# Mamba-2 layer in one kernel: other shapes for two TensorE products, a new order on every engine, and loads with a wait for each group

## The chip, the cores and the metric

The kernel runs on one core of one Trainium2 chip. The metric is the device time of that core in microseconds, from one launch.

## The reference

Two sequences of 4096 tokens, 256 wide (`x`, float32), go through a layer norm without weights; the result `xn` feeds two branches, and `x` is added to both:

```
zxbcdt = xn @ W_in                       # 256 -> 512 (z) + 768 (x, B, C) + 8 (dt)
xBC = silu(causal_conv(xBC, 4 taps))     # x: 8 heads of 64; B, C: 128 each
dt = softplus(dt + dt_bias); a = -exp(A_log)
y = ssd(x * dt, dt * a, B, C) + x * D    # the state space recurrence
y = y * silu(z); y = y * rsqrt(mean(y*y) + eps) * rms_w
h = xn + y @ W_out                       # 512 -> 256
branch1 = layernorm(h) * ln_g + ln_b
branch2 = tanh(xn @ F1 @ F2 @ F3 + bias)
out = x + branch1 + branch2
```

The reference cuts the recurrence into chunks of 64; the kernel uses chunks of 128 tokens, with the same result.

## The kernel before, in words

A step is 128 tokens of both sequences (`q` = 0 and 1), so there are 32 steps. Each engine has a program of its own; they meet at semaphores. Every program is a function `one_pass(k, b)` with the operations of several steps in an order written out by hand: step `k+2` is loaded and its statistics taken, `k+1` projected, `k` and `k-1` in the recurrence, `k-2` finished. Passes run from k = -2 to 33, the middle ones in a loop. An engine does its operations strictly in that order, and waits where one isn't ready.

For a step, TensorE transposes `xn` (`transpose_x`), projects the second branch and dt (`branch_project`), the six tiles of convolution channels (`conv_project`, ct = 0 to 5) and z (`z_project`). These are float32r products: each operand is split into a high and a low part, and three products of one pass each are summed (`split_products`). Everything else on TensorE is plain float32; one such matmul stands in the trace as two instructions. `ring0` and `ring1` are the two PSUM banks through which the projections go, so that each projection waits until an earlier one has been read: `z_project(k, 0)` for the taps of tile 3, `conv_project(k, 4)` for those of tile 1.

VectorE adds three of the four convolution taps (`tap`, L624), computes softplus of 16 columns in steps of one small instruction each (`softplus(k, b, i)`, L637 to L659, the series of `log1p` with `LOG_TERMS` terms; the last step writes `a_wide` and increments `a_done`), and the chunk's elementwise work: `weigh` (L677), `scale_off` (L683), `new_state` (L689), `add_diag` (L694), `apply_gate` (L698), `last_h` (L705). In the order before, the softplus steps stand one by one between large instructions. `sums` on TensorE waits for `a_done`; ScalarE's `sums`, VectorE's `low_rows`, GpSimd's `spread_rows` and TensorE's `exponents` follow from it.

Inside a chunk, `y_diag` multiplies for each of 8 heads the 128x128 weights `mm` (stationary) with 64 columns of `xdt` (moving) into `yd_bank`, tokens on the partitions. `x_tokens` turns x to tokens, ScalarE copies it to `xsb`, and `x_times_dt` makes `xdt` in 8 instructions. GpSimd makes `xw`, the skip term `xd = x * D`, adds it (`add_skip`, L467), decays the state, masks, and does the inverse square roots and the output (L491, L493). After the gate, `transpose_y` turns y, ScalarE copies it to `yts` (L916), and `out_project` multiplies it with `wo` in float32.

Ahead of the passes come 16 loads and the constants: all are issued by the SP queue, and VectorE, ScalarE, TensorE and GpSimd each first wait until every load but those of `x` has landed (`s_load` >= 16 * 17). Then the weights are split, F1 @ F2 @ F3 is multiplied out, and the tables of the exponents (`left`, `right`) are filled by VectorE. Only then does VectorE begin with the norm of step 0.

Of the kernel before, what the change touches and what calls it, by code (L numbers as in the profile page):

```python
# [29 lines left out]
P = 128  # L30
# [25 lines left out]
LOG_TERMS = 6  # L56
# [11 lines left out]
def program(nc, x, w_in, conv_w, conv_b, dt_bias, a_log, d_skip, rms_w, w_out, ln_g, ln_b,  # L68
# [6 lines left out]
    with ExitStack() as ctx:  # L75
# [6 lines left out]
        def sems(name, n):  # L82
# [3 lines left out]
        ring0, ring1, e_bank0, e_bank1, xt_bank, bg_bank, yoff_bank, yd_bank = [  # L86
            ctx.enter_context(nc.psum_tensor(n, [P, 512], F32))
            for n in ("ring0", "ring1", "e_bank0", "e_bank1", "xt_bank", "bg_bank", "yoff_bank", "yd_bank")]
# [6 lines left out]
        lay2 = sb("lay2", [P, 4 * Q * DI])  # L95
# [6 lines left out]
        mask = lay2[:, 0:QUAD * P].rearrange("p (j t) -> p j t", t=P)  # L102
        pair = lay2[:, QUAD * P:2 * QUAD * P].rearrange("p (j t) -> p j t", t=P)
        sel = lay2[:, 2 * QUAD * P:2 * QUAD * P + Q * H]
        f3s = lay2[:, 2 * QUAD * P + Q * H:2 * QUAD * P + Q * H + nf].rearrange("p (k n) -> p k n", k=KD)
        f23 = lay2[:, 2 * QUAD * P + Q * H + nf:2 * QUAD * P + Q * H + 2 * nf].rearrange("p (k n) -> p k n", k=KD)
# [3 lines left out]
        wo = sb("wo", [P, KI, D])  # L110
        rmsw = sb("rmsw", [P, KI])
# [3 lines left out]
        d_bc = sb("d_bc", [P, H])  # L115
        lng = sb("lng", [P, D])
# [40 lines left out]
        w16 = sb("w16", [P, Q * H])  # L157
# [3 lines left out]
        xsb = sb("xsb", [P, Q, DI])  # L161
# [7 lines left out]
        t1, t2, yg = (lay2[:, i * Q * DI:(i + 1) * Q * DI].rearrange("p (q n) -> p q n", q=Q) for i in range(3))  # L169
        junk = sb("junk", [P, Q, DI])  # L170
        ss = sb("ss", [P, Q])
        sse = sb("sse", [P, Q])
        rr = sb("rr", [P, Q])
        yts = sb("yts", [P, Q, KI, P])
# [8 lines left out]
        s_load = sem("s_load")  # L183
        s_gp = sem("s_gp")
        s_const = sem("s_const")
        s_high = sem("s_high")
        s_sel = sem("s_sel")
        s_split = sem("s_split")
# [11 lines left out]
        f_in_psum, f_read, z_in_psum, zt_done, gate_done = (sems(n, Q) for n in ("f_in_psum", "f_read", "z_in_psum", "zt_done", "gate_done"))  # L200
        c_in_psum, u_done = (sems(n, CT) for n in ("c_in_psum", "u_done"))
        th_done, xs_done = (sems(n, NG) for n in ("th_done", "xs_done"))
        tap_done = sems("tap_done", CT)
        halo_done, relu_done, ee_done = map(sem, ("halo_done", "relu_done", "ee_done"))
        soft = sem("soft")
        a_done, res_chain, res_done = map(sem, ("a_done", "res_chain", "res_done"))
        sums_in_psum, sums_read, rows_done, spread_done, w16_done, total_done = map(
            sem, ("sums_in_psum", "sums_read", "rows_done", "spread_done", "w16_done", "total_done"))
        (xt2_in_psum, xsb_done, xdt_done, xw_done, xd_done, sdec_done, bg_in_psum, bg_read, yoff_in_psum, t1_done,
         t2_done, st_in_psum, state_done, g_done, yd_in_psum, y_done, yg_done, ss_done, sse_done, rr_done, yt_in_psum, yts_done,  # L210
         o_in_psum, h_done, st2_done, mv2_done, ve2_done, rs2_done, shift2_done, hn_done, hg_done, out_done) = (
            sems(n, Q) for n in (
                "xt2_in_psum", "xsb_done", "xdt_done", "xw_done", "xd_done", "sdec_done", "bg_in_psum", "bg_read",
                "yoff_in_psum", "t1_done", "t2_done", "st_in_psum", "state_done", "g_done", "yd_in_psum", "y_done", "yg_done",
                "ss_done", "sse_done", "rr_done", "yt_in_psum", "yts_done", "o_in_psum", "h_done", "st2_done",
                "mv2_done", "ve2_done", "rs2_done", "shift2_done", "hn_done", "hg_done", "out_done"))
        e_in_psum, e_done, m_done = ([sems(f"{n}{q}_", 2) for q in range(Q)] for n in ("e_in_psum", "e_done", "m_done"))

        def begun(step):

            return not isinstance(step, int) or step >= 0

# [47 lines left out]
        def _(sp):  # L270
# [6 lines left out]
            for j in range(BUF):  # L277
                load(j, j, slice(j * P, (j + 1) * P))
            loads = [
                (win[:, :, :], w_in.rearrange("(k p) n -> p k n", p=P)),  # L280
                (f1s[:, :, :], f1t.rearrange("(k p) n -> p k n", p=P)),
                (f2s[:, :, :], f2t.rearrange("(k p) n -> p k n", p=P)),
                (f3s[:, :, :], f3.rearrange("(k p) n -> p k n", p=P)),
                (wo[:, :, :], w_out.rearrange("(k p) n -> p k n", p=P)),
                (rmsw[:, :], rms_w), (cw[:, :, :], conv_w.rearrange("(k p) n -> p k n", p=P)), (cb[:, :], conv_b),
                (a_neg[:, 0:H], a_log.partition_broadcast(P)),
                (a_neg[:, H:2 * H], a_log.partition_broadcast(P)), (d_bc[:, :], d_skip.partition_broadcast(P)),
                (lng[:, :], ln_g.partition_broadcast(P)), (lnb[:, :], ln_b.partition_broadcast(P)),
            ]
            for dst, src in loads:  # L290
                sp.dma_start(dst, src).then_inc(s_load, 16)
            sp.wait_ge(s_gp, 1)
            for row in (0, LO):
                sp.dma_start(brow[row:row + 1, 0:D], f_bias.rearrange("(a n) -> a n", a=1)).then_inc(s_load, 16)
                sp.dma_start(brow[row:row + 1, D:FB], dt_bias.rearrange("(a n) -> a n", a=1)).then_inc(s_load, 16)
# [4 lines left out]
            def one_pass(k, b, loads_on=True):  # L300
                b1 = (b + 1) % BUF
                if live(k + 1) and loads_on and live(k + 1 + BUF):
                    sp.wait_ge(res_done, k + 2)
                    load(k + 1 + BUF, b1, rows_of(k + 1 + BUF))
                if live(k - 1):
                    sp.wait_ge(out_done[0], k)
                    sp.wait_ge(out_done[1], k)
                    bo = (b - 1) % BUF
                    sp.dma_start(out_t[rows_of(k - 1), :, :], obuf[:, bo]).then_inc(stored[bo], 16)
# [12 lines left out]
        n_loads = 13 + 4  # L322


        @block.gpsimd
        def _(pool):
# [6 lines left out]
            g.memset(nhalf[:, :], -0.5).then_inc(s_gp, 1)  # L333
            g.memset(a_wide[:, :], 0.0).then_inc(s_gp, 1)
# [45 lines left out]
            pool.wait_ge(s_load, 16 * n_loads)  # L380
            pool.wait_ge(s_split, 1)

            def layer_norm_scale(k):
                pool.wait_ge(mv1_done, k + 1)
# [865 lines left out]
```

## Time and profile before

| | us |
|---|---|
| median of 3 runs | 858.38 |
| lowest, highest | 854.18, 859.85 |
| profiled execution | 857.2 |
| its span in the trace | 855.5 |

The profiled execution is 1.7 us longer than the span that the trace shows, and 1.2 us under the median. Its granted TensorE clock was 0.976 of full speed over the span. Of the engines' rows below, a busy time counts an instruction from its start to its end; neighbours on one engine overlap a little, so what an instruction costs in a row of them is the distance from start to start.

### The profile page before, as it was taken

Reading aid. Unit: us, or ns where it says so; the run is one execution under the profiler, and the core shown is the slowest. Engines: PE = TensorE matmul, PEld = TensorE weight load, DVE = VectorE, ACT = ScalarE, POOL = GpSimd, SP = SyncE. Lnnn points to the kernel's source line nnn. Section 1 sums busy time; section 2 is a strip of 40 time slices with the busy share of each in tenths; the row PEclk is TensorE's granted clock in tenths of the full one; section 3 lists DMA queues with packets and bytes.
Section 4 is the critical chain, followed back from the end, with each engine's and each line's share of the span. In section 5 each row is a group of like instructions: output and inputs, shape, how many; then the busy total and the mean of one; then the engine's idle time right before and its main releaser. Section 6 shows DMA issues by size and latency. Waiting matters only on the chain.

```text
span 855.5 us, 18389 instructions
## 1 busy us (share of the span) xinstructions
PE 800.8 (94%) x4944; PEld 671.5 (78%) x4944; DVE 726.5 (85%) x1826; ACT 681.3 (80%) x1767; POOL 702.0 (82%) x1096
## 2 busy tenths in 40 slices
PE   1479999999999999999999999999999999999974
PEld 1368888888888888888888888888888888888753
DVE  1669899998999999899999999999999998998741
ACT  1169888898888888988888889888888898888841
POOL 4036888898888889988888899888888988888884
PEclk9689999999999999999999999999999999999986
DMA  5000000000000000000000000000000000000000
GB/s 174 0 1 13 14 26 26 26 11 14 25 25 25 25 25 25 6 19 25 25 25 25 25 25 1 24 25 25 25 25 25 25 0 24 25 25 13 14 13 25
DMA packets 20848, 19.98 MB, mean 23 GB/s; under 512 B 2646, under 2 KB 20568, under 8 KB 20824
## 3 DMA queue, kind: packets, MB, share of 16 engines
q1 hardware_dynamic: 20824, 19.71, 7.2%
q8 instruction: 10, 0.16, 0.1%
q14 instruction: 14, 0.11, 0.0%
HBM read 11.31 MB, written 8.39 MB: 23 GB/s over the span
## 4 chain that ended last, share of the span: by engine, by line
POOL 39%; DVE 25%; issue 17%; PE 13%; ACT 2%; SPq 2%; POOLq 1%; DVEq 1%; DMA 0%; ACTq 0%
DVE u L624 7%; POOL xw L446 7%; PE ring L1012 5%; POOL obuf L491 4%; POOL left L434 3%; POOL sdec L453 3%; POOL xd L461 3%; POOL rs L483 3%; DVE pa L646 3%; POOL right L430 3%; DVE lay L677 3%; POOL obuf L493 3%; POOL btg L441 2%; DVE lay L683 2%; PE yoff_bank L1149 2%
## 5 line engine op out<-in xcount | busy, mean ns | idle before, releaser
L624 DVE SCALAR_TENSOR_TENSOR u<-ring,cw,u 128x256 f32<-128x256 f32 x576 | 260.5, 469 | 30.4 <-ACT u L847 29.8
L1012 PE MATMUL ring<-xhl,wh 128*128 128x262 f32 x768 | 174.8, 319 | 3.4 <-DVE u L624 3.4
L1012 PE MATMUL ring<-wh,xhl 128*128 128x512 f32 (+1 forms) x512 | 164.1, 374 | 3.3 <-DVE u L624 3.3
L1012 PEld LDWEIGHTS ring<-xhl,wh 128*128 128x128 f32 x768 | 124.7, 193 | 43.6 <-DVE u L624 21.6
L847 ACT ACTIVATE u<-ring,cb,cw 128x256 f32<-128x256 f32 x192 | 107.9, 562 | 45.6 <-PE ring L1012 40.9
L907 ACT ACTIVATE xdt<-xsb,dts 128x64 f32<-128x64 f32 x512 | 128.5, 335 | 0.0
L1131 PE MATMUL yd_bank<-xdt,lay 128*128 128x64 f32 x1024 | 123.2, 274 | 0.9 <-ACT yts L916 0.9
L1149 PE MATMUL yoff_bank<-wo,yts 128*128 128x256 f32 x512 | 122.1, 382 | 1.1 <-ACT yts L916 0.7
L1131 PEld LDWEIGHTS yd_bank<-xdt,lay 128*128 128x128 f32 x1024 | 121.2, 194 | 1.7 <-ACT yts L916 1.3
L1012 PE MATMUL ring<-xhl,wl 128*128 128x262 f32 x384 | 110.2, 287 | 0.0
L1012 PEld LDWEIGHTS ring<-wh,xhl 128*128 128x128 f32 x512 | 93.9, 192 | 20.0 <-issue 7.2
L1149 PEld LDWEIGHTS yoff_bank<-wo,yts 128*128 128x128 f32 x512 | 93.9, 192 | 13.9 <-issue 2.7
L860 ACT ACTIVATE xs<-u 128x512 f32<-128x512 f32 x96 | 60.2, 627 | 45.8 <-DVE u L624 45.5
L677 DVE SCALAR_TENSOR_TENSOR lay<-e_bank,btg 128x512 f32<-128x512 f32 x128 | 86.7, 678 | 1.3 <-POOL btg L441 0.4
L1012 PE MATMUL ring<-wl,xhl 128*128 128x264 f32 (+1 forms) x256 | 87.8, 343 | 0.0
L467 POOL TENSOR_TENSOR lay<-lay,xd 128x512 f32<-128x512 f32 x64 | 81.6, 1276 | 0.0
L891 ACT ACTIVATE e_bank<-e_bank 128x512 f32<-128x512 f32 x128 | 75.4, 590 | 0.3
L1012 PEld LDWEIGHTS ring<-xhl,wl 128*128 128x128 f32 x384 | 73.6, 192 | 0.0
L1112 PE MATMUL yoff_bank<-state,xs 128*128 128x512 f32 x128 | 68.4, 616 | 1.6 <-DVE hh L705 1.3
L491 POOL TENSOR_TENSOR obuf<-hh,lng 128x256 f32<-128x256 f32 x64 | 46.5, 727 | 28.4 <-ACT hh L897 28.4
L705 DVE SCALAR_TENSOR_TENSOR hh<-yoff_bank,rr,xn 128x256 f32<-128x256 f32 x64 | 30.5, 477 | 44.8 <-POOL rr L474 38.4
L1100 PE MATMUL e_bank<-right,left 128*128 128x512 f32 x128 | 66.6, 522 | 1.4 <-POOL left L434 1.4
(134 smaller groups left out, 1995.7 us busy)
## 6 DMA issues: line engine op xcount, KB each, us to landing
xin<-in_x_dram SPq DMA_DIRECT2D x32, 256.0 KB, 2.9
out_dram<-obuf SPq DMA_DIRECT2D x32, 256.0 KB, 2.8
lay<-in_w_in_dram SPq DMA_DIRECT2D x1, 1288.0 KB
wo<-in_w_out_dram SPq DMA_DIRECT2D x1, 512.0 KB
lay<-in_f1t_dram SPq DMA_DIRECT2D x1, 256.0 KB
lay<-in_f2t_dram SPq DMA_DIRECT2D x1, 256.0 KB
lay<-in_f_dram SPq DMA_DIRECT2D x1, 256.0 KB
lng<-in_ln_g_dram SPq DMA_DIRECT2D x1, 128.0 KB
```

The costliest lines, as they stand in the source:

```text
L467: g.tensor_tensor(t2[:, q], t1[:, q], xd[:, q], ALU.add).then_inc(t2_done[q], 1)
L491: g.tensor_tensor(obuf[:, b, q], hh[:, q], lng[:, :], ALU.mult).then_inc(hg_done[q], 1)
L624: v.scalar_tensor_tensor(out=u[:, ct], in0=conv_bank(ct)[:, :, t:t + P], scalar=cw[:, ct, t:t + 1], in1=u[:, ct], op0=ALU.mult, op1=ALU.ad ...
L677: v.scalar_tensor_tensor(out=mm[:, q, hs], in0=e_bank[half][:, :].rearrange("p (j t) -> p j t", t=P), scalar=1.0, in1=btg[:, q, P:2 * P].u ...
L847: s.activation(u[:, ct], conv_bank(ct)[:, :, HALO:PH], ACT.Identity, bias=cb[:, ct:ct + 1], scale=cw[:, ct, HALO:TAPS]).then_inc(u_done[ct ...
L891: s.activation(e_bank[half][:, :], e_bank[half][:, :], ACT.Exp).then_inc(e_done[q][half], 1)
L907: last = s.activation(xdt[:, q, head], xsb[:, q, head], ACT.Copy, scale=dts[:, b, q * H + h:q * H + h + 1])
L1012: last = mul(out, a, c, start=first and i == 0, stop=i == n - 1)
L1100: mul(bank[:, :], left[:, 2 * q + half], right[:, :, :].rearrange("p j t -> p (j t)"), start=True, stop=True)\
L1112: mul(yoff_bank[:, :], xs[:, b, KI + 1, q], state[:, q], start=True, stop=True).then_inc(yoff_in_psum[q], 1)
L1131: last = mul(yd_bank[:, h * HD:(h + 1) * HD], mm[:, q, h], xdt[:, q, h * HD:(h + 1) * HD], start=True, stop=True)
L1149: last = mul(yoff_bank[:, 0:D], yts[:, q, ki], wo[:, ki], start=ki == 0, stop=ki == KI - 1)
```

## The change

- `y_diag` has the operands exchanged: 64 columns of `xdt` are stationary and the 128 columns of `mm` moving. Even heads write partitions 0 to 63 of `yd_bank`, odd heads 64 to 127, so that y has channels on the partitions. ScalarE copies it (`y_copy`), GpSimd adds the skip term there (`xs` times `d_ch`, a column of D), and four transposes (`y_tokens`) turn it back to tokens in `yd_bank`.
- `xsb` and its copy are gone: `x_times_dt` reads PSUM, `scale_x` scales `xdt`; `w16` is gone.
- `out_project` takes split operands: `woh`, `wol`, `yts` (high) and `ytl` (low), 12 one-pass products where there were 4 float32 ones. VectorE makes `ytl` (`y_low`).
- `LOG_TERMS` is 5, not 6. `branch` on ScalarE handles both q at once; GpSimd's `rms_scale`, `last_norm_scale` and `output` too.
- The orders of all engines are new. VectorE's softplus steps 0 to 9 of a step follow each other directly, and so do the three taps of a tile.
- Loads: step 0's `x` first, then F2, F3, the convolution part of W_in, F1, the z part, the other `x`, W_out, ln; the small ones are issued by ScalarE's queue. Each consumer waits for its own group. Step 0's norm, transposition and split stand ahead of the constants on every engine; `left` is filled by ScalarE.

```
-LOG_TERMS = 6
+LOG_TERMS = 5
...
             def y_diag(k, q):
                 if begun(k - 1 + q):
-                    pe.wait_ge(yts_done[1 - q], k + q)
+                    pe.wait_ge(ytl_done[1 - q], k + q)
...
-                    last = mul(yd_bank[:, h * HD:(h + 1) * HD], mm[:, q, h], xdt[:, q, h * HD:(h + 1) * HD],
+                    half = slice(h % 2 * HD, (h % 2 + 1) * HD)
+                    last = mul(yd_bank[half, h // 2 * P:(h // 2 + 1) * P], xdt[:, q, h * HD:(h + 1) * HD], mm[:, q, h],
                                start=True, stop=True)
+                last.then_inc(yc_in_psum[q], 1)
+
+            def y_tokens(k, q):
+                pe.wait_ge(t2_done[q], k + 1)
+                for ki in range(KI):
+                    last = tr(yd_bank[:, ki * P:(ki + 1) * P], yct[:, q, ki * P:(ki + 1) * P], ident[:, :])
                 last.then_inc(yd_in_psum[q], 1)
...
+                pairs = []
                 for ki in range(KI):
-                    last = mul(yoff_bank[:, 0:D], yts[:, q, ki], wo[:, ki], start=ki == 0, stop=ki == KI - 1)
+                    pairs += [(yts[:, q, ki], woh[:, ki]), (yts[:, q, ki], wol[:, ki]), (ytl[:, q, ki], woh[:, ki])]
+                last = split_products(yoff_bank[:, 0:D], pairs)
...
+            def y_low(k, q):
+                dve.wait_ge(yts_done[q], k + 1)
+                bank = yd_bank[:, :].rearrange("p (k t) -> p k t", k=KI)
+                v.tensor_tensor(ytl[:, q], bank, yts[:, q].bitcast(F32), ALU.subtract).then_inc(ytl_done[q], 1)
...
+            def y_copy(k, q):
+                act.wait_ge(yc_in_psum[q], k + 1)
+                s.activation(yct[:, q], yd_bank[:, :], ACT.Copy).then_inc(yc_done[q], 1)
...
             def add_skip(k, q):
-                pool.wait_ge(t1_done[q], k + 1)
+                pool.wait_ge(yc_done[q], k + 1)
                 pool.wait_ge(xd_done[q], k + 1)
-                g.tensor_tensor(t2[:, q], t1[:, q], xd[:, q], ALU.add).then_inc(t2_done[q], 1)
+                g.tensor_tensor(yct[:, q], yct[:, q], xd[:, q], ALU.add).then_inc(t2_done[q], 1)
```

The new orders, cut to the part of a pass of which the prediction speaks. TensorE: `branch_project(k+1, 1)`, `branch_project(k+1, 0)`, `transpose_y(k-1, 0)`, `b_and_g(k, 1)`, `states(k-1, 1)`, `exponents(k, 1, 1)`, `conv_project(k+1, 2)`, `y_diag(k-1, 1)`, `conv_project(k+1, 0)`, `x_tokens(k, 1)`, and then the next pass with `sums`. ScalarE: `branch(k+1)`, `y_channels(k-1, 0)`, `square(k-1, 0)`, `b_and_g(k, 1)`, `softplus_exp(k+1)`, `last_apply(k-2, 1)`, `conv_in(k+1, 2)`, `y_copy(k-1, 1)`. VectorE: `low_part(k+1)`, `last_stats(k-2, 0)`, `last_mean_var(k-2, 0)`, `add_diag(k-1, 0)`, `apply_gate(k-1, 0)`, `last_mean_var(k-2, 1)`, `weigh(k, 0, 1)`, `scale_off(k-1, 1)`, `weigh(k, 0, 0)`, `y_low(k-1, 0)`, `new_state(k-1, 1)`, `softplus(k+1, 0 to 9)`, then nine taps of tiles 2, 0 and 3 with `norm_stats`, `add_diag(k-1, 1)` and `apply_gate(k-1, 1)` among them, two taps of tile 1, `last_h(k-1, 0)`, the third tap, `low_rows`, `y_low`, `scale_off`, `weigh`, `new_state`, the taps of tiles 4 and 5, `last_h(k-1, 1)`, `norm_apply(k+2)`. GpSimd: `mask_g(k, 0)`, `decay_state(k, 0)`, `residual_bias(k-1)`, `last_norm_scale(k-2)`, `add_skip(k-1, 1)`, `output(k-2)`.

## Rows read from the trace of the kernel before

**Rows 1.** Busy times of the engines over the span, from the page.

```profile
PE 800.8 (94%) x4944; PEld 671.5 (78%) x4944; DVE 726.5 (85%) x1826; ACT 681.3 (80%) x1767; POOL 702.0 (82%) x1096
```

**Rows 2.** Busy time by window: one steady step, and the loads.

```profile
2.00:10.00 8.00, 0.00 (x0) 0.00 (x0) 0.00 (x0) 0.09 (x1) 7.03 (x30) 1.00 0.91 298
...
400.00:424.50 24.50, 24.48 (x156) 20.52 (x156) 22.52 (x57) 21.04 (x57) 21.73 (x34) 1.00 0.07 21
```

**Rows 3.** Timeline of TensorE's matmuls over one steady step.

```profile
400.17 0.41 PE L1012 MATMUL ring<-xhl,wh 128*128 128x262 f32 x2
...
400.90 0.39 PE L1100 MATMUL e_bank<-right,left 128*128 128x512 f32 x1
...
402.72 1.89 PE L1149 MATMUL yoff_bank<-wo,yts 128*128 128x256 f32 x8
404.44 0.27 PE L1090 MATMUL bg_bank<-ident,xs 128*128 128x128 f32 x1
...
408.54 0.60 PE L1081 MATMUL xt_bank<-ident,xs 128*128 128x128 f32 x4
408.90 0.49 PE L1012 MATMUL ring<-xhl,wh 128*128 128x262 f32 x2
...
415.53 1.90 PE L1131 MATMUL yd_bank<-xdt,lay 128*128 128x64 f32 x16
417.26 0.35 PE L1069 MATMUL bg_bank<-a_wide,upto 128*128 128x16 f32 x2
...
424.71 0.40 PE L1012 MATMUL ring<-xhl,wh 128*128 128x262 f32 x2
```

**Rows 4.** Timeline of VectorE in the same step.

```profile
406.66 0.47 DVE L624 SCALAR_TENSOR_TENSOR u<-ring,cw,u 128x256 f32<-128x256 f32 x1
...
407.17 0.48 DVE L624 SCALAR_TENSOR_TENSOR u<-ring,cw,u 128x256 f32<-128x256 f32 x1
...
409.75 0.99 DVE L646 SCALAR_TENSOR_TENSOR pa<-pa,ww 128x16 f32<-128x16 f32 x1
410.66 1.26 DVE L624 SCALAR_TENSOR_TENSOR u<-ring,cw,u 128x256 f32<-128x256 f32 x3
...
417.26 0.69 DVE L615 TENSOR_TENSOR xhl<-ring,xhl 128x512 fp32r<-128x512 f32 x1
417.87 0.69 DVE L694 TENSOR_TENSOR yd_bank<-yd_bank,lay 128x512 f32<-128x512 f32 x1
```

**Rows 5.** Timeline of GpSimd in the same step.

```profile
409.43 1.27 POOL L410 TENSOR_TENSOR res<-res,lnb 128x512 f32<-128x512 f32 x1
```

**Rows 6.** Groups of instructions by line and form, VectorE and ScalarE.

```profile
L646 DVE SCALAR_TENSOR_TENSOR pa<-pa,ww 128x16 f32<-128x16 f32 x96 | 59.6, 621 | 0.0
...
L659 DVE TENSOR_TENSOR a_wide<-dts,a_neg 128x64 f32<-128x64 f32 x32 | 17.6, 551 | 0.0
L637 DVE SCALAR_TENSOR_TENSOR den<-ee 128x16 f32<-128x16 f32 x32 | 16.1, 504 | 3.1
...
L916 ACT ACTIVATE yts<-yd_bank 128x512 f32<-128x512 f32 x64 | 37.7, 589 | 5.1 <-PE yd_bank L1138 5.1
```

**Rows 7.** Timeline of VectorE in an early pass, GpSimd idle.

```profile
53.96 0.17 DVE L650 SCALAR_TENSOR_TENSOR pb<-pa,sv 128x16 f32<-128x16 f32 x1
54.16 0.17 DVE L653 SCALAR_TENSOR_TENSOR dts<-pb,relu 128x16 f32<-128x16 f32 x1
```

**Rows 8.** Timeline of the start, all engines.

```profile
8.89 2.79 SPq L291 DMA_DIRECT2D cb<-in_conv_b_dram  x1
...
16.96 0.22 ACT L816 ACTIVATE a_neg<-a_neg 128x16 f32<-128x16 f32 x1 [14.87 <-DMA brow<-in_dt_bias_dram]
...
17.09 1.47 ACT L818 ACTIVATE wh<-lay 128x1536 fp32r<-128x1536 f32 x1
...
35.06 0.59 PE L1055 MATMUL ring<-bias_r,ones_r 128*128 128x264 f32 x1 [1.48 <-DVE xhl L615]
...
40.85 0.17 DVE L637 SCALAR_TENSOR_TENSOR den<-ee 128x16 f32<-128x16 f32 x1
```

More of the change, by code:

```diff
@@ L495, in one_pass @@
+            ahead.append(0)
             def one_pass(k, b):
@@ L577, in _ @@
-            for ki in range(KI):
-                v.tensor_scalar(wo[:, ki], wo[:, ki], rmsw[:, ki:ki + 1], None, ALU.mult)
-            for m, bank in enumerate((ring0, ring1)):
-                dve.wait_ge(s_fhigh, m + 1)
-                last = v.tensor_tensor(wl[:, m, FC:FC + D], bank[:, 0:D], wh[:, m, FC:FC + D].bitcast(F32), ALU.subtract)
-            last.then_inc(s_split, 1)
-            dve.wait_ge(s_split, 2)
+            ahead = []
             def norm_stats(k, b):
+                if at_start(k) and ahead:
+                    return
@@ L603, in norm_apply @@
             def norm_apply(k, b):
+                if at_start(k) and ahead:
+                    return
                 if begun(k - BUF):
@@ L612, in low_part @@
             def low_part(k, b):
+                if at_start(k) and ahead:
+                    return
                 dve.wait_ge(xh_done, k + 1)
@@ new lines, in _, with low_weights @@
+            norm_apply(0, 0)
+            dve.wait_ge(l_conv, 16)
+            v.tensor_copy(wh[:, :, FC + D:FC + FB], win[:, :, DI + CONV:DI + CONV + H]).then_inc(h_small, 1)
+            dve.wait_ge(l_bias, 64)
+            v.tensor_copy(bias_r[:, :], brow[:, :]).then_inc(h_small, 1)
+            low_part(0, 0)
+            ahead.append(0)
+            def low_weights(at, n, of):
+                for kd in range(KD):
+                    last = v.tensor_tensor(wl[:, kd, at:at + n], win[:, kd, of:of + n], wh[:, kd, at:at + n].bitcast(F32), ALU.subtract)
+                return last
@@ L1152, in one_pass @@
+            pe.wait_ge(s_const, 1)
+            transpose_x(0, 0)
+            ahead.append(0)
+            pe.wait_ge(l_f1, 16)
+            pe.wait_ge(s_f23s, KD)
+            for m, bank in enumerate((yoff_bank, yd_bank)):
+                for kd in range(KD):
+                    last = mul(bank[:, 0:D], f1s[:, kd, m * P:(m + 1) * P], f23[:, kd], start=kd == 0, stop=kd == KD - 1)
+                last.then_inc(s_f123, 1)
             def one_pass(k, b):
                 b1, bo = (b + 1) % BUF, (b - 1) % BUF
+                if live(k):
+                    sums(k)
@@ L1196, in one_pass @@
                 if live(k - 1):
-                    y_diag(k - 1, 0)
+                    y_tokens(k - 1, 0)
                 if live(k):
-                    sums(k)
+                    b_and_g(k, b, 0)
+                    exponents(k, 0, 0)
+                if live(k - 1):
+                    y_off(k - 1, bo, 1)
                 if live(k + 1):
```

694 lines of the change are left out of this document (370 added, 324 removed).

## The prediction

> **What bounds the kernel now.** I read the engines' busy times first. TensorE stands at 94% [rows 1], but a matmul's row overlaps its neighbour, so that alone says little. The window over one steady step says more: in 24.50 us TensorE shows 24.48, VectorE 22.52, GpSimd 21.73, ScalarE 21.04 [rows 2]. The same matmul comes back after 24.54 us (400.17 to 424.71) [rows 3]; 32 steps of that are 785 us, and the rest of the 855.5 us is start and end. Adding up TensorE's timeline from start to start gives about 23.7 us of work in a step and 0.8 us of waits. So TensorE is the bound, VectorE 2 us behind it. A change that takes 2 us from TensorE and puts 1.5 us on VectorE changes the bound, and that is what this one does.
>
> The start is a second matter. Nothing but constants runs until the last small load has landed at 16.96, the first projection is at 35.06, the first softplus at 40.85 [rows 8].
>
> **TensorE, part by part.** `out_project` takes 404.44 - 402.72 = 1.72 us [rows 3]. The 12 products that replace it have 256 columns in one pass; the nearest row is six products of 262 columns in 0.73 us (400.17 to 400.90) [rows 3], 0.122 each, so 1.46 us. Twice a step: -0.5 us.
> `y_tokens` is four more transposes, 0.36 us (408.54 to 408.90) [rows 3], twice: +0.7 us.
> `y_diag` takes 1.73 us, 16 instructions of 0.108 (415.53 to 417.26) [rows 3]. Afterwards each streams 128 columns, not 64. Float32 streams 256 columns in 1.72 / 8 = 0.215 us [rows 3], so 128 take 0.107: if the heads still follow each other, the cost stays at 1.7. If the two halves of the array work side by side, it is about 0.9 and -1.7 us for the step. No row shows a matmul on half the array, so these are the ends. I take the lower one with 0.6.
> The Trainium skill (TensorEngine Tiling (Array Packing), Key Properties) says that tiles of the array work independently and in parallel; its factor of two for 64 columns would give the 0.9.
> Sum: 23.7 - 0.5 + 0.7 - 1.7 = 22.2 us, or 23.9 without the overlap.
>
> **VectorE.** From its 22.5 us busy [rows 2]:
> - `y_low` reads a bank and subtracts, like L615: 0.61 us from start to start (417.26 to 417.87) [rows 4], twice: +1.2.
> - Dependent neighbours. A tap that follows another costs 0.39 to 0.42 when it needn't wait (1.26 for three) [rows 4]. One that needs the tap before it starts 0.51 later (406.66 to 407.17) [rows 4]. The old order put something else between; the new one makes ten taps and both `apply_gate` follow what they need: 12 x 0.12 = +1.5.
> - The softplus chain. Between large instructions a small one costs about 0.1; in a chain it costs 0.20 (53.96 to 54.16) [rows 7]. Ten of them: +1.0, less 0.1 for the term that is dropped. The chain takes about 2.1 us.
> - What goes: holds by GpSimd. The 16-column instruction at 409.75 took 0.99 us instead of 0.17, and ended at 410.74, as GpSimd's instruction ended (409.43 + 1.27 = 410.70) [rows 4, 5]. The means say that this is the rule: 621 ns for `pa`, 504 for `den`, 551 for `a_wide` [rows 6] against some 165, 175 and 220. That is 3 x 0.46 + 0.33 + 0.33, about 2 us a step, and it goes if the chain falls where GpSimd is idle.
> Sum: 22.5 + 1.2 + 1.5 + 0.9 - 2.0 = 24.1 us. VectorE becomes the bound, even if TensorE falls to 22.2.
>
> **The path through both.** After a step's `a_done`, VectorE needs about 14.2 + 1.1 us to `norm_apply(k+2)` without a pause, TensorE then 0.5 for `transpose_x`, 0.2 until it is seen, ScalarE 0.65 for the split; VectorE has only 0.95 of other work in that time and stands for 0.3 to 0.4. From `low_part` to the next `a_done` are 7.7 us. The loop is 24.2 to 24.4 us: forecast 24.3, 0.2 under now. If the heads don't overlap, `transpose_x` comes later and TensorE's 23.9 and its waits give about 24.8.
> ScalarE loses the `xsb` copies and gains `y_copy` of the same size (589 ns) [rows 6]; GpSimd's work falls by about 1 us. Neither is late in this account, except in the rival below. The read of PSUM by `x_times_dt` I take at the old cost; up to 0.05 more on 16 instructions, 0.8 us, would lie in ScalarE's 3 us of slack; it could gain nothing either.
>
> **The start.** The loads moved at 298 GB/s [rows 2]; `x`, F2, F3 and the convolution part of W_in are 1.6 MB, so they are there at 2 + 5.3 = 7 to 8 us, not 17. On ScalarE's queue the eight small loads cost what they cost SP, 2.8 us for `cb` alone [rows 8] and some 7 in all, so ScalarE's first work is at about 9; that wait is covered by the landing of the weights. It splits W_in (1.47 us [rows 8]), VectorE makes the low part; with the transposes at 12 and the product of the F's, the branch's projection starts at about 16 to 17 in place of 35.06, and the first softplus at about 21 to 24 instead of 40.85 [rows 8]. `left` on ScalarE (3 us) now lies ahead of its first `branch` and is in this. I take -18 us, from -14 (ScalarE's queue held up longer) to -20. The last steps have no cover either way: 0, give or take 3.
>
> **The sum.** 857.2 - 18 - 29 x 0.2 (the passes that run at the full period) = 833.4; the median lies 1.2 above the profiled execution: 834.6, say 835.
>
> **Rivals.**
> (1) VectorE loses less than I charge: the neighbours overlap and the period is 23.6, because TensorE's 22.2 leaves room. Then -18 - 27 = 813. Against it: the 0.51 between dependent taps is measured.
> (2) The chain collides with GpSimd: slower. Count from the end of `branch_project(k+1, 0)`. ScalarE's `branch`, `y_channels`, `square`, `b_and_g` and the exponential are done at +2.5, VectorE's `new_state(k-1, 1)` at +2.7, so the chain runs from +2.75 to +4.8. `y_diag(k-1, 1)` ends at +3.6 (with the overlap), `y_copy` takes 0.59 [rows 6], and GpSimd starts `add_skip`, 1.27 us as in [rows 5], at +4.35. The last two steps of the chain are due at +4.4 and +4.6. One that comes behind `add_skip` ends with it, +1.0 us; if both do, the second meets `output` and it is +2.1. TensorE's `sums` waits for it, and all of TensorE behind `sums`. The period is then 25.3 or 26.4, the time 864 or 896. It decides by 0.1 to 0.3 us, finer than my account. For it: every number above; against it: without the overlap `y_diag` ends 0.8 later, and the chain is through.
> The Trainium skill (SBUF — State Buffer, Who interferes with whom) has the rule: a VectorE instruction with two inputs in SBUF and a GpSimd instruction that reads SBUF exclude each other for the whole instruction, and the first to issue wins. By that rule nine of the chain's ten instructions can be held, and the trace agrees.
> (3) The TensorE halves don't overlap: period 24.8, time 858.4 - 18 + 8 = 848.
> (4) The start doesn't gain, because ScalarE's queue is held up until the loads have landed as SP's was: 10 us less, 845 with the forecast's period.
>
> **How the numbers follow.** A change of 1% is about what can be told from none here: 849.8 and 867.0 are the bounds. Chances: the forecast with the halves or without (825 to 850, so rivals 3 and 4 are in it) 0.50, of which 0.03 lies above 849.8; rival 1 0.17; rival 2 with one hold (850 to 876) 0.19, of which 0.07 is over 867; with two 0.11; the rest 0.03. Faster 0.64, same 0.16, slower 0.20. The range 806 to 876 leaves out two holds and the fastest cases, under 0.2.
>
> **What would show it.** The first softplus near 21 to 24 us. TensorE's new `y_diag` near 0.9 us from first to last start, `out_project` 1.46. VectorE's busy time in a steady step over 23.5 us and above all others. The distance from one `sums` to the next. In the chain, instructions of 0.17 us and a `pa`, `dts` or `a_wide` near 1 us only if rival 2 holds. I am wrong if TensorE still has no idle time in a step, or if a wait on ScalarE or GpSimd that I have not counted exceeds 1 us.

## The result and the profile after

The changed kernel takes 947.15 us (944.58 to 949.21, 4 runs), the kernel before 856.77 us beside it: a ratio of 1.105 (95% interval 1.100 to 1.110). It is slower by 90 us; 835 was forecast.

The engines' busy times, as in [rows 1], and a window as long as a usual step, as in [rows 2]:

```profile
PE 802.5 (85%) x5456; PEld 654.5 (69%) x5456; DVE 841.6 (89%) x1855; ACT 675.1 (71%) x1680; POOL 644.2 (68%) x841
...
400.00:427.45 27.45, 24.07 (x168) 20.23 (x168) 25.57 (x56) 20.08 (x51) 19.67 (x25) 0.94 0.06 19
```

VectorE went from 726.5 us to 841.6, TensorE stayed at 802 and now has over 3 us a step in which it does nothing. `den`, the chain's first instruction, comes back every 27.45 us (24.4 to 24.6 before). In 12 of the 31 distances it is 28.45 to 29.68, together 16.7 us over the usual one; TensorE's clock was at the half level in part of each of those. Over the span it was at the half level for 71.7 us (40.3 before). The window shown and the rows below lie in two of the long steps, 28.72 and 28.50; `dts` and `a_wide` are held as long in the others, and the two `xn` take 1.5 to 1.6 us there for 1.96 here.

VectorE around the chain, and further down in the step:

```profile
404.81 0.16 DVE L614 SCALAR_TENSOR_TENSOR den<-ee 128x16 f32<-128x16 f32 x1
...
406.55 1.21 DVE L630 SCALAR_TENSOR_TENSOR dts<-pb,relu 128x16 f32<-128x16 f32 x1
407.80 1.24 DVE L636 TENSOR_TENSOR a_wide<-dts,a_neg 128x64 f32<-128x64 f32 x1
...
424.27 1.96 DVE L583 TENSOR_SCALAR xn<-xin,mv,rs 128x256 f32<-128x256 f32 x2
```

GpSimd in the same step; in [rows 5] it ran beside a `pa`:

```profile
406.46 1.27 POOL L472 TENSOR_TENSOR yct<-yct,xd 128x512 f32<-128x512 f32 x1 [2.36 <-ACT yct L952]
407.68 1.27 POOL L504 TENSOR_TENSOR obuf<-hh,lng 128x512 f32<-128x512 f32 x1
...
423.98 1.05 POOL L448 TENSOR_TENSOR xw<-xdt,exs 128x512 f32<-128x512 f32 x1 [0.39 <-ACT xdt L939]
424.99 1.09 POOL L455 TENSOR_TENSOR sdec<-state,exs 128x512 f32<-128x512 f32 x1
```

The chain starts at 404.81 and does eight steps in 1.74 us. `dts` is issued at 406.55, 0.09 us after `add_skip` (L472, 406.46), and ends where that ends: 1.21 us for what takes 0.17. `a_wide` then finds `output` (L504), issued at 407.68, and ends where that ends: 1.24 us. At 424.27 the two `xn` of `norm_apply` meet `xw` and `sdec` in the same way: 1.96 us for two (the first ends 0.15 us behind `xw`, the second 0.15 behind `sdec`). `dts` is issued 0.08 to 0.11 us behind `add_skip` in 29 of the 32 steps, all but the first three, and is held in each of those. The groups by form say the same; the columns are count, busy us and mean ns:

```profile
L583 DVE TENSOR_SCALAR xn<-xin,mv,rs 128x256 f32<-128x256 f32 x64 | 53.9, 881 | 2.7 <-POOL rs L393 0.9
...
L636 DVE TENSOR_TENSOR a_wide<-dts,a_neg 128x64 f32<-128x64 f32 x32 | 36.5, 1141 | 1.1
L630 DVE SCALAR_TENSOR_TENSOR dts<-pb,relu 128x16 f32<-128x16 f32 x32 | 35.5, 1110 | 1.1
```

Before, `a_wide` took 551 ns [rows 6], `dts` 169 and `xn` 401 on the mean.

TensorE in the same step, as in [rows 3]:

```profile
404.64 1.09 PE L1195 MATMUL yd_bank<-lay,xdt 128*64 128x128 f32 x16
405.66 0.52 PE L1067 MATMUL ring<-xhl,wh 128*128 128x262 f32 x2
...
409.08 0.40 PE L1130 MATMUL bg_bank<-a_wide,upto 128*128 128x16 f32 x2 [1.98 <-DVE a_wide L636]
...
411.12 0.42 PE L1067 MATMUL ring<-xhl,wl 128*128 128x262 f32 x1
...
421.86 0.37 PE L1067 MATMUL yoff_bank<-woh,yts 128*128 128x256 f32 x1
...
423.32 0.39 PE L1163 MATMUL e_bank<-right,left 128*128 128x512 f32 x1
...
426.28 0.66 PE L1060 MATMUL ring<-ident,xn 128*128 128x128 f32 x4 [1.18 <-DVE xn L583]
```

`y_diag` takes 405.66 - 404.64 = 1.02 us instead of 1.73, `out_project` 423.32 - 421.86 = 1.46. But `sums` waits 1.98 us for `a_wide`, and `transpose_x` 1.18 for `xn`. The `ring` product at 411.12 shows 0.42 where the one before the wait (406.02) shows 0.28: there the granted clock is 0.50 (from 410.2 to 413.4), 1.2 GHz and not 2.4. The wait for `a_wide` is as long in the usual steps, which have no such stretch. The sum of the waits over the span:

```profile
PE bg_bank L1130 <- DVE a_wide L636: 60.5, 32, 2.0
...
PE ring L1060 <- DVE xn L583: 36.7, 32, 1.4
```

The start, as in [rows 8], did what it was meant to:

```profile
5.58 0.75 DVE L562 BATCH_NORM_STATS2 st<-xin 128x6 f32<-128x256 f32 x2 [5.58 <-DMA xin<-in_x_dram]
...
18.39 0.40 PE L1116 MATMUL ring<-bias_r,ones_r 128*128 128x264 f32 x1 [2.72 <-DVE wl L746]
...
22.30 0.18 DVE L614 SCALAR_TENSOR_TENSOR den<-ee 128x16 f32<-128x16 f32 x1
```

The first `den` is at 22.30 in place of 40.85, 18.55 us earlier. So the 90 us are a gain of 18 at the start and a loss of 109 in the steps.

### The profile page after: what moved, and what is told of

Its sections match the earlier page's. It is cut to its first block and busy times, and to the rows that moved or that the text cites. A ratio compares the mean times of both kernels' runs of the same rounds, so it can differ in the third digit from the quotient of the medians.

```text
span 946.0 us, 19099 instructions
## 1 busy us (share of the span) xinstructions
PE 802.5 (85%) x5456; PEld 654.5 (69%) x5456; DVE 841.6 (89%) x1855; ACT 675.1 (71%) x1680; POOL 644.2 (68%) x841
## 5 line engine op out<-in xcount | busy, mean ns | idle before, releaser
L472 POOL TENSOR_TENSOR yct<-yct,xd 128x512 f32<-128x512 f32 x64 | 82.2, 1284 | 79.4 <-ACT yct L952 79.4
L939 ACT ACTIVATE xdt<-xt_bank,dts 128x64 f32<-128x64 f32 x512 | 111.6, 337 | 0.1
L1067 PEld LDWEIGHTS ring<-wh,xhl 128*128 128x128 f32 x512 | 92.7, 189 | 18.4 <-DVE u L601 5.2
L481 POOL TENSOR_TENSOR rr<-ss,nhalf 128x2 f32<-128x2 f32 x32 | 22.5, 702 | 100.3 <-issue 99.4
L1067 PE MATMUL yoff_bank<-woh,yts 128*128 128x256 f32 x256 | 82.9, 324 | 1.4 <-DVE ytl L694 1.4
L448 POOL TENSOR_TENSOR xw<-xdt,exs 128x512 f32<-128x512 f32 x64 | 67.1, 1049 | 16.4 <-ACT xdt L939 15.5
L1067 PE MATMUL yoff_bank<-wol,yts 128*128 128x256 f32 x256 | 76.5, 299 | 0.0
L1067 PE MATMUL yoff_bank<-woh,ytl 128*128 128x256 f32 x256 | 76.0, 297 | 0.0
L1195 PE MATMUL yd_bank<-lay,xdt 128*64 128x128 f32 x1024 | 70.0, 279 | 4.1 <-DVE ytl L694 4.1
L466 POOL TENSOR_TENSOR xd<-xs,d_ch 128x512 f32<-128x512 f32 x64 | 66.6, 1042 | 8.5 <-POOL left L434 5.1
L455 POOL TENSOR_TENSOR sdec<-state,exs 128x512 f32<-128x512 f32 x64 | 68.3, 1067 | 0.0
```

The lines of the kernel that those rows point to most:

```text
L448: g.tensor_tensor(heads(xw[:, q]), heads(xdt[:, q]), per_head(exs[:, b, Q * H + q * H:Q * H + (q + 1) * H]), ALU.mult)\
L455: g.tensor_tensor(heads(sdec[:, q]), heads(state[:, q]), per_head(exs[:, b, 2 * Q * H + q * H:2 * Q * H + (q + 1) * H]), ALU.mult)\
L466: g.tensor_tensor(xd[:, q].rearrange("p (c t) -> p c t", c=KI), xs[:, b, 0:KI, q], d_ch[:, :].unsqueeze(2).to_broadcast([P, KI, P]), ALU.m ...
L472: g.tensor_tensor(yct[:, q], yct[:, q], xd[:, q], ALU.add).then_inc(t2_done[q], 1)
L939: last = s.activation(xdt[:, q, head], xt_bank[:, head], ACT.Copy, scale=dts[:, b, q * H + h:q * H + h + 1])
L1067: last = mul(out, a, c, start=first and i == 0, stop=i == n - 1)
```

## The experiments

Unless it says otherwise, each is the changed kernel with the edit shown, and "period" is the usual distance from one `den` to the next. No edit leaves an operation out.

**1. The chain without GpSimd beside it.** `add_skip`, and with it `output` behind it, waits until the softplus chain is through.

```
                 if live(k - 1):
+                    if live(k + 1):
+                        pool.wait_ge(a_done, k + 2)
                     add_skip(k - 1, 1)
```

> One wait added to the changed kernel: GpSimd's add_skip(k-1, 1) waits until the softplus chain of step k+1 has ended (a_done). Theory A (the port lock): dts and a_wide, 1.11 and 1.14 us in the changed kernel, fall to about 0.17 and 0.22, the usual period falls from 27.45 to about 25.4, and the periods with the TensorE clock at its lower level become fewer; the time is about 880 us. Theory B (the chain is slow by its own dependences, and TensorE would wait anyway): the two stay near 1.1 us and the added wait makes it the same or some 10 us slower, 947 to 960 us.

Measured: 870.25 us (869.05 to 872.37), 1.0135 of before (1.011 to 1.016), period 25.39. One wait more on GpSimd takes 77 us away. The groups by form:

```profile
L585 DVE TENSOR_SCALAR xn<-xin,mv,rs 128x256 f32<-128x256 f32 x64 | 49.7, 816 | 2.7 <-POOL rs L393 0.9
...
L638 DVE TENSOR_TENSOR a_wide<-dts,a_neg 128x64 f32<-128x64 f32 x32 | 7.2, 224 | 1.1
...
L632 DVE SCALAR_TENSOR_TENSOR dts<-pb,relu 128x16 f32<-128x16 f32 x32 | 5.6, 174 | 1.1
```

`dts` and `a_wide` together are 1.85 us shorter, the period 2.06, and the long periods are gone too: 30.6 us at the half level. Thirty periods of 2.06 are 62 us; the rest is the clock (16.7 us by the long periods), to 2 us. `xn` is still held.

**2. Only the second of the two holds taken away.** The same wait, placed between `add_skip` and `output`.

```
                     add_skip(k - 1, 1)
+                if live(k + 1):
+                    pool.wait_ge(a_done, k + 2)
                 if live(k - 2):
                     output(k - 2, b1)
```

> As e1, but the wait for a_done stands behind add_skip(k-1, 1) and ahead of output(k-2). Theory A (each hold is one GpSimd instruction long, and they add): dts stays at 1.1 us, held by add_skip; a_wide falls to 0.22. The period is 26.4 us, midway between 27.45 and 25.39, the time about 900 us. Theory B (what counts is that GpSimd works at all in the chain, or the late add_skip itself): the period is that of the changed kernel, 27.4, or that of e1, 25.4.

Measured: 926.38 us (924.18 to 928.13), ratio 1.079 (1.077 to 1.082). `dts` takes 1106 ns, `a_wide` 225. The periods repeat 26.41, 27.75, 27.72, where the long ones hold a stretch at the half level; over the span 84.4 us. So the holds are worth 1.0 us a period each (25.39, 26.41, 27.45). The time is over what 26.41 would give, because two of three periods are lengthened by the clock.

**3. The norm on ScalarE.** `norm_apply` becomes two activations with a shift and a scale that GpSimd works out, ahead of `conv_silu(k+1, 2)` and `z_silu(k+1, 1)`; the holds of the chain remain.

```
+            def norm_apply(k, b):            # ScalarE; gone from VectorE
+                act.wait_ge(shift1_done, k + 1)
+                for q in range(Q):
+                    last = s.activation(xn[:, b, q], xin[:, b, q], ACT.Identity, bias=shift1[:, q:q + 1], scale=rs1[:, q:q + 1])
+                last.then_inc(xn_done, 1)
```

> norm_apply of every step but the first is done by ScalarE (two activations with scale and bias, two more small GpSimd instructions per step) in the changed kernel. Theory A (VectorE's xn, 0.88 us each in place of 0.40, is held by GpSimd, and sits on the way to transpose_x): the period falls by the two holds, 0.96 us, and by 0.6 us of VectorE's work, to about 26 us, and the time to about 905 us. Theory B (only the chain's holds matter, the path through xn has slack): the same time within 1%, 940 to 955 us.

Measured: 951.23 us (949.7 to 953.55), ratio 1.108 (1.106 to 1.111), periods 27.72, 27.77, 28.1 and 29.05 in turn: nothing gained, although VectorE lost 1.8 us of busy time a step. ScalarE's timeline:

```profile
424.48 1.09 ACT L875 ACTIVATE xn<-xin,shift,rs 128x256 f32<-128x256 f32 x2 [0.45 <-DVE hh L709]
425.48 0.62 ACT L911 ACTIVATE xs<-u 128x512 f32<-128x512 f32 x1
426.00 0.58 ACT L916 ACTIVATE gate<-ring 128x512 f32<-128x512 f32 x1
426.48 0.58 ACT L882 ACTIVATE xhl<-ring 128x512 fp32r<-128x512 f32 x1
```

`xn` can't start before `last_h` of an older step (`hh`) has read the buffer that it writes, and the split (`xhl`) stands behind `xs` and `gate`: it is at 426.48, 27.48 us after the step's `low_part` at 399.00; in the changed kernel's step it was 27.86 (399.11 to 426.97). VectorE, free earlier, waits for it: 58.2 us over the span against 17.0. The clock took what was left: from the fourth on every period holds a stretch at the half level (149.8 us over the span), and from the end of `a_wide` to `xn` are 15.2 to 16.5 us, where run 4, which has the same orders on VectorE and ScalarE and no such stretch in its usual steps, shows 14.61. Work taken from VectorE behind a buffer and a fixed order on ScalarE gains little.

**4. Both.** Edits 1 and 3 together.

> Both edits at once. Theory A: the holds add, the period is that of the account without holds, 24.3 us or less (23.7 if VectorE's 0.6 us counts), the time 815 to 840 us, under both kernels. Theory B (a further bound lies close behind, such as ScalarE's order or the 24 us of VectorE): the period stays above 25, the time above 860 us.

Measured: 859.81 us (858.01 to 862.28, 10 runs), ratio 1.0018 (1.0005 to 1.0032), period 25.09. Beside edit 1 the norm on ScalarE is worth 10 us, 0.30 a period; where the chain is held and the clock falls in every step, it was worth nothing.

**5. The other hold moved as well.** With edit 1, GpSimd's `scale_x(k, 0)` (the `xw` of the timeline) waits for `norm_apply`, and the operations behind it change places a little: `residual` now comes behind `mask_g` and `decay_state`, and `residual_bias` behind `last_norm_scale`.

```
                     state_weights(k, b)
+                    if live(k + 1):
+                        pool.wait_ge(xn_done, k + 2)
                     scale_x(k, b, 0)
```

> e1, and GpSimd's scale_x(k, 0) also waits for xn_done of step k+1; behind it GpSimd's order is decay_state, mask_g, decay_state, residual, last_norm_scale, residual_bias. VectorE does the norm as in the changed kernel. Theory A (the hold of xn, 0.82 in place of 0.40 each, is on the path): xn falls to 0.40, the period from 25.39 to 24.5, the time from 870 to about 844 us. Theory B (slack on that path, as e2 may say): the period stays at 25.2 to 25.4, 865 to 872 us.

Measured: 856.06 us (854.46 to 857.76, 10 runs), ratio 0.9975 (0.9964 to 0.9986), period 24.95 (one in three 25.03). Its `xn` and the window of a step:

```profile
L587 DVE TENSOR_SCALAR xn<-xin,mv,rs 128x256 f32<-128x256 f32 x64 | 23.5, 410 | 2.7 <-POOL rs L393 0.9
...
400.00:424.95 24.95, 24.00 (x172) 19.35 (x171) 23.09 (x58) 20.61 (x52) 19.67 (x26) 1.00 0.07 21
```

The holds of `dts`, `a_wide` and `xn` are gone, and the period is still 0.65 above my 24.3. Two `xn` lose 0.87 us against edit 1, and only 0.44 comes off the period. The rest comes back at one place, between `low_part` (L596) and `a_wide` (L640). VectorE, and ScalarE ahead of it:

```profile
410.21 0.73 DVE L587 TENSOR_SCALAR xn<-xin,mv,rs 128x256 f32<-128x256 f32 x2
...
412.32 0.69 DVE L596 TENSOR_TENSOR xhl<-ring,xhl 128x512 fp32r<-128x512 f32 x1 [0.45 <-ACT xhl L870]
...
417.18 0.69 DVE L698 TENSOR_TENSOR ytl<-yd_bank,yts 128x512 fp32r<-128x512 f32 x1 [0.26 <-ACT yts L962]
...
418.39 0.23 DVE L618 SCALAR_TENSOR_TENSOR den<-ee 128x16 f32<-128x16 f32 x1
...
420.40 0.22 DVE L640 TENSOR_TENSOR a_wide<-dts,a_neg 128x64 f32<-128x64 f32 x1
```

```profile
415.91 0.60 ACT L879 ACTIVATE ft<-ring 128x512 f32<-128x512 f32 x1 [0.60 <-POOL res L409]
```

The guard and the later place make GpSimd's `residual` (`res`) late, ScalarE's `branch` (`ft`) waits 0.60 us for it (18.4 us over the span, nothing in run 1), `yts` stands behind `ft`, and `y_low` (`ytl`) waits for `yts`; and `den` now meets `residual_bias` (222 ns for 163). From `low_part` to the end of `a_wide` are 420.62 - 412.32 = 8.30 us, 7.87 in run 1: the edit itself costs 0.43.

**6. The dependent neighbours apart.** With both guards, VectorE's taps and `apply_gate` no longer follow what they need; tiles 2 and 0 alternate, for instance.

```
-                    tap(k + 1, 2, 0)
-                    tap(k + 1, 2, 1)
-                    tap(k + 1, 2, 2)
-                    tap(k + 1, 0, 0)
...
+                    tap(k + 1, 2, 0)
+                    tap(k + 1, 0, 0)
+                    tap(k + 1, 2, 1)
+                    tap(k + 1, 0, 1)
```

> e6, and VectorE's order with no tap behind the one it needs (tiles 2 and 0 alternate, tile 3 is mixed with apply_gate and norm_mean_var) and none of the two apply_gate directly behind add_diag: ten of the twelve dependent neighbours are gone. Theory A (each costs 0.12 us and VectorE is the bound): the period falls by about 1.0 us against e6, to 23.5 to 23.8, the time to 815 to 825 us. Theory B (they overlap with waits that are there anyway, or TensorE is the bound): within 0.3 us of e6's period.

Measured: 858.61 us (856.21 to 861.03, 10 runs), ratio 1.0003 (0.9988 to 1.0018), period 24.91 to 24.96. VectorE is busy for 22.62 us in the window of a step, 0.47 less than in run 5, and what it gained turned into waits: VectorE's `add_diag` now waits 0.48 us for `y_tokens` (L1210) and a tap 0.33 for ScalarE's `u`, and TensorE's `z_project` waits for the third tap, which alternating makes later. From the end of `a_wide` to `xn` are 14.53 us, as in run 5. Two lines of the waits, which the run before doesn't have in that size:

```profile
PE ring L1075 <- DVE u L605: 27.9, 34, 1.6
...
DVE yd_bank L676 <- PE yd_bank L1210: 22.7, 32, 3.3
```

**7. `y_diag` without the overlap.** The four even heads first, then the four odd ones, so that neighbours lie in the same half of TensorE. `y_diag` also waits for both halves of `mm` before its first head, where the changed kernel waits for the second half ahead of head 4; GpSimd waits for nothing new.

```
-                for h in range(H):
+                for h in (0, 2, 4, 6, 1, 3, 5, 7):
```

> The changed kernel with y_diag's heads in the order 0, 2, 4, 6, 1, 3, 5, 7: four in a row on one half of the array, then four on the other. Theory A (the 1.02 us of the new y_diag is two neighbours side by side on the halves): without alternation it is back at 16 x 0.107 = 1.7 us. Theory B (the instruction itself became cheaper, the weights being 64 columns): it stays near 1.0 us.

Measured: 885.66 us, one run beside before's 858: about 61 us faster than the changed kernel, with a slower `y_diag`. TensorE, VectorE and GpSimd:

```profile
406.08 1.58 PE L1195 MATMUL yd_bank<-lay,xdt 128*64 128x128 f32 x16
407.59 0.51 PE L1067 MATMUL ring<-xhl,wh 128*128 128x262 f32 x2
...
408.00 0.18 DVE L630 SCALAR_TENSOR_TENSOR dts<-pb,relu 128x16 f32<-128x16 f32 x1
408.21 0.23 DVE L636 TENSOR_TENSOR a_wide<-dts,a_neg 128x64 f32<-128x64 f32 x1
...
408.38 1.28 POOL L472 TENSOR_TENSOR yct<-yct,xd 128x512 f32<-128x512 f32 x1 [2.83 <-ACT yct L952]
```

`y_diag` takes 407.59 - 406.08 = 1.51 us. It ends half a microsecond later against the chain, `y_copy` and `add_skip` with it, and `a_wide` is issued at 408.21, 0.17 ahead of `add_skip` at 408.38. `y_diag` itself starts where it did, 0.2 us ahead of `den`. The period is 25.90. This is the collision from the other side: no wait was added to GpSimd, only TensorE was made slower. (`xn`, at 972 ns, is held longer than in run 1, and the period is 0.5 us over that run's.)

**8. The same, with both guards.** Where nothing is held, what is the overlap worth?

> The changed kernel with both guards on GpSimd (add_skip behind the end of the softplus chain, the scaling of xdt behind norm_apply; 856.1 us, period 24.95) and, besides, y_diag going over the four even heads first and then over the four odd ones, so that neighbours lie in the same half of TensorE and each y_diag takes about 1.5 us and not 1.02. Theory A: with the holds gone TensorE has room (some 2 us of waits in a period), and the period grows by less than the 1.0 us added: up to 25.3, 867 us or less. Theory B: y_diag lies on the path that closes the loop, and the period grows by the whole 1.0: 25.95, about 887 us.

Measured: 862.12 us (860.55 to 862.78, 8 runs), ratio 1.0052 (1.0036 to 1.0069), period 25.06 to 25.18.

```profile
400.00:425.08 25.08, 24.77 (x172) 20.30 (x171) 23.17 (x58) 20.57 (x53) 19.66 (x26) 1.00 0.07 21
```

TensorE has 24.77 us of rows in 25.08, against 24.00 in 24.95 with the overlap. About 1.0 us more of `y_diag` costs 0.13 us a period, between the end of `a_wide` and `xn` (14.67 for 14.53). TensorE was not what set the period of the new order.

**9. The new start alone.** The kernel before in all its orders of the steps, with the new loads, the wait for each group, and step 0's norm ahead of the constants (the diff's start, with `left` still filled by VectorE).

```
-            dve.wait_ge(s_load, 16 * n_loads)
...
+            norm_stats(0, 0)
+            norm_mean_var(0)
...
+            norm_apply(0, 0)
+            dve.wait_ge(l_conv, 16)
```

> The kernel before with the new start alone: loads in order of need on two queues, a wait per group, the first step's norm ahead of the constants, left filled by ScalarE. Steady orders and products as before. Theory A (the start gives what it shows, first softplus at 22 in place of 41 us): 857 - 18 = 839 us, period 24.5 unchanged. Theory B (part of it is given back, because the early passes then wait or the clock is low for longer): 845 to 857 us.

Measured: 841.88 us (840.2 to 843.76), ratio 0.9801 (0.9776 to 0.9827); first `den` at 24.2, period 24.5. This version beats both kernels: 17 us under before (859.12 beside it), 105 under the changed one.

**10. One of the TensorE savings in the old order.** To the version of 841.9 us I added `out_project` in 12 products, with `y_low`; VectorE's `y_low(k-1, 0)` stood behind two taps of tile 0.

```
                     tap(k + 1, 0, 1)
                     softplus(k + 1, b1, 2)
+                if live(k - 1):
+                    y_low(k - 1, 0)
```

> The kernel before with the new start (the version that took 841.9 us, steady period 24.5) and, of the three TensorE savings, only out_project in 12 one-pass products instead of 4 float32 ones, with the y_low that it needs on VectorE, put where the order before has work that doesn't depend on it; the series keeps its six terms. Theory A: the order before is bound by TensorE, so the 0.52 us of two out_projects come off each period: 24.0, about 826 us. Theory B: the 1.2 us of y_low bring VectorE (22.5 busy, with holds) up to about 23.7, and new waits between the engines take the 0.5 back: 24.5, about 842. Theory C: y_diag and out_project now wait for y_low, which stands behind large instructions, and a period of over 25 results: 858 or more.

Measured: 957.24 us (955.41 to 958.98, 5 runs), ratio 1.117 (1.115 to 1.120): 115 us more than without it, for an edit that takes 0.52 us of work from TensorE and adds 1.2 to VectorE. TensorE:

```profile
404.67 0.39 PE L1160 MATMUL bg_bank<-xs 128*128 128x128 f32 x2
407.63 2.33 PE L1202 MATMUL yd_bank<-xdt,lay 128*128 128x64 f32 x16 [2.58 <-DVE ytl L711]
...
410.73 0.42 PE L1075 MATMUL ring<-xhl,wl 128*128 128x262 f32 x1
```

`y_diag` waits 2.58 us, because the bank that it overwrites is read by `y_low`; behind it the clock is at the half level (0.42 for a product of 0.28; 155.4 us of half level over the span, against 25.1).

**11. The same instruction five places earlier.**

```
                     softplus(k + 1, b1, 0)
+                if live(k - 1):
+                    y_low(k - 1, 0)
```

> As the run with the new start and out_project in 12 products (957 us, period about 27.5 to 29), but y_low of the first sequence stands five VectorE instructions earlier, right behind the first softplus step, where yts has just been written. There y_diag waited 2.58 us for y_low (from 404.78 to 407.63), ring and taps behind it. Theory A: the place of this one instruction is what cost 100 us: y_diag then starts about 1.2 us after the matmul ahead of it, the half-clock stretch behind it is gone, and the period is 24.5 to 25.2, 842 to 865 us. Theory B: any y_low between the copy and y_diag breaks the order, and it stays over 900.

Measured: 864.04 us (861.0 to 865.32, 4 runs), ratio 1.0068 (1.005 to 1.009), period 24.8 to 25.15. One instruction's place was worth 93 us. The line of the waits, first of run 10 and then of this one:

```profile
PE yd_bank L1202 <- DVE ytl L711: 81.3, 32, 4.0
```

```profile
PE yd_bank L1202 <- DVE ytl L711: 30.9, 32, 1.8
```

50 of the 93 us are this wait; the half level falls from 155.4 to 29.7 us, and I put the other 43 down to that, which no run isolates.

**12. The wait covered.** Besides, `y_diag(k-2, 1)` moved behind `exponents(k-1, 0, 0)` and `conv_project(k, 3)`.

> As the run before it in this call, and y_diag of the second sequence moved behind the first exponents and conv_project of tile 3, work of 0.31 + 0.72 us that doesn't need y_low and that covers the wait. Theory A (the order before is bound by TensorE): TensorE loses 0.52 us of work a period and has no new wait: 24.0, 826 us. Theory B: VectorE's 1.2 us are the new bound (22.4 + 1.2 and its waits): 24.5 or more, 842 or more.

Measured: 886.02 us (884.95 to 888.74, 4 runs), ratio 1.033 (1.031 to 1.035), period 25.0 to 25.3 with five of 28.7 to 29.1, each with a stretch at the half level. The `exponents` were put forward to where they now wait themselves:

```profile
407.90 0.39 PE L1160 MATMUL bg_bank<-xs 128*128 128x128 f32 x2
409.66 0.49 PE L1171 MATMUL e_bank<-right,left 128*128 128x512 f32 x1 [1.38 <-POOL left L436]
```

The 0.52 us of `out_project` didn't show in any of the three. Its rows are as computed, but the old order gave it back each time as another wait. Whether another order would keep it wasn't tried.

## Why the prediction was wrong

The step that failed is the term of -2.0 us in VectorE's sum, the holds by GpSimd ("it goes if the chain falls where GpSimd is idle"), and with it the 2.1 us at which the chain went into the loop. The chain doesn't fall where GpSimd is idle. Held, it takes 4.22 us in the changed kernel, and 2.17 in run 1, where it is not: 2.05 us a period, on the path. Runs 1, 2 and 7 show both holds and their price.

The prediction had this as **rival 2 with two holds**, with a chance of 0.11. It put `add_skip` at +4.35 and the last two steps of the chain at +4.4 and +4.6. In the trace, counted from 401.89, where TensorE goes on behind `branch_project`, `add_skip` comes at +4.57 and `dts` at +4.66. The count was 0.2 to 0.3 us early for both, and right to 0.05 in what mattered, the distance between them. The mistake was to give the side that it pointed to (two holds) a fifth of the chance of the forecast. The rival's 896 us was also too low, by 51: its period of 26.4 was 1.05 too short, and it had no term for the clock.

The loop that the prediction describes is the one that closes in the changed kernel and in runs 1 and 5: through the first two stretches VectorE has no wait over 0.13 us in a usual step but the 0.18 for its own statistics and, in run 5, the 0.26 for `yts`. The stretches, in us:

| stretch | prediction | changed kernel | run 1 | run 5 |
|---|---|---|---|---|
| `low_part` to the end of `a_wide` | 7.7 | 9.92 | 7.87 | 8.30 |
| from there to the end of the second `xn` | 15.3 | 16.16 | 16.14 | 15.27 |
| from there to the next `low_part` | 1.35 | 1.38 | 1.38 | 1.38 |
| sum | 24.35 | 27.46 | 25.39 | 24.95 |

- **The hold of `xn`.** Not in the prediction. I had looked for small instructions that GpSimd might hold and passed over `xn`, a large one, which the new order puts beside `xw` and `sdec`. It costs 16.14 - 15.27 = 0.87 us a period; run 5 shows 0.44 of it in the period, because its edit costs 0.43 elsewhere, 14 us in all (870.25 to 856.06). The Trainium skill (SBUF — State Buffer, Who interferes with whom) lists tensor_scalar among the operations that can take the shared pair of ports, besides those with two inputs, under conditions on its operands. The trace agrees, with 881 ns for 401.
- **The clock.** Not in the prediction either: 16.7 us by the changed kernel's long periods, and perhaps over a third of run 10's loss. In the order before TensorE waits little in a step, and nothing there led me to price what a wait costs behind it.
- **VectorE 24.1 us, and a loop of 24.2 to 24.4.** Right in mechanism and nearly in size. With nothing held and no cost of that edit the three stretches are 7.87 + 15.27 + 1.38 = 24.52, though no run had all three at once; 0.17 of the difference lies between `low_part` and `a_wide`. The 23.09 us busy of run 5 leave out the gaps between dependent neighbours; its period less VectorE's three waits (0.45, 0.26, 0.18) is 24.1. But VectorE is not alone as a bound: run 6 takes its dependent neighbours apart, a term that I had at 1.5 us, and other waits fill what comes free.
- **`out_project` 1.46 us**: as measured. **`y_diag` 0.9 with the overlap**: 1.02, and the overlap is real, since the same products cost 1.51 one half after the other. But 1.51 is not my 1.7 either, so rival 3's price was too high. Its time, 848, was wrong for a better reason: a longer `y_diag` keeps `add_skip` out of the chain, but `xn` stays held (run 7: 885.66).
- **TensorE as a bound at 22.2**: its waits, not its work, fill the step (24.07 of rows in 27.45, a half-clock stretch in it).
- **The start, -18**: right. The first `den` is 18.55 us earlier in the changed kernel, and in the old order the same start is worth 17.2 us of the time (859.12 to 841.88). Rivals 1 and 4 fell.

So the sum is 835 + (2.05 + 0.87 + 0.2) x 30 + 17 = 946; 947 was measured. The 0.2 is the loop's 24.52 over the forecast's 24.3; the terms for the holds are from the runs, and the 17 is what the long periods have over the usual one.

## What to carry to other kernels

When two engines can exclude each other, write down which instructions stand side by side in the new order, with both starts; if they are nearer than the account is good for, the collision is the forecast, or the order is not finished. A wait on the offending engine at the one place (run 1) is cheap and settles it; look for what the delayed instructions then hold up, since run 5's edit gave half of its gain back. In the order before, the chain was spread out, one step between large instructions, and some 2 us of holds a step left TensorE 24.48 us of rows in 24.50; gathered in front of a wait of another engine, each hold is on the path. And in an order written by hand, a saving on one engine has to be followed to the next wait: here a start of its own was worth 17 us, and none of the savings inside the steps that were tried was worth anything.

## What the runs showed of the hardware

- A VectorE instruction of 16 columns (0.17 us) takes 1.21 us when it is issued 0.09 us behind a GpSimd instruction of 512 columns that reads SBUF, and 0.18 when it is issued 0.38 ahead (408.00 against 408.38 in run 7); `a_wide`, 0.17 ahead there, takes 0.23.
- `xn`, a float32 instruction with one large input and two columns of scalars, is held in the same way: 881 ns on the mean beside GpSimd, 410 with GpSimd held back.
- Not every GpSimd instruction holds. In the kernel before, the second `xn` (issued at 414.58) and `pb` are issued while `rs` runs, one column and 0.63 us as profiled, and take 0.40 and 0.16 us; so do all 30 `xn` issued behind the start of an `rs` and ahead of its end (397 to 409 ns). "For the whole instruction", as the prediction has it, fits GpSimd's instructions of 512 columns and not this one. VectorE, then GpSimd:

```profile
414.26 0.72 DVE L608 TENSOR_SCALAR xn<-xin,mv,rs 128x256 f32<-128x256 f32 x2
414.90 0.16 DVE L650 SCALAR_TENSOR_TENSOR pb<-pa,sv 128x16 f32<-128x16 f32 x1
```

```profile
414.44 0.63 POOL L483 TENSOR_TENSOR rs<-ve,nhalf 128x1 f32<-128x1 f32 x1
```

- Eight heads of 64 channels (one `y_diag`) on alternating halves of TensorE cost 1.02 us; one half after the other, 1.51; the form before, 64 columns moving on the whole array, 1.73.
- After waits of 1.98 us (12 of the changed kernel's 31 steps, though nearly all have the wait), 2.58 (run 10) and 1.1 to 1.6 (run 12, in five steps of 31, though nearly all have such a wait) TensorE was found at the half level in the products that followed, and a step with such a stretch is 1.0 to 4.0 us longer than its neighbours.
